# W0 product moved into the first gather's tiles, second layer's weights behind the second gather

## The reference, cut to what matters

```
n    = ln(x)                                             # (6250, 256)
agg  = segment_sum((n @ W_r[type])[src] / deg[type, dst], dst)
x1   = x + agg + n @ W0.T + W0_b                         # first graph layer
x2   = x1 + moe(ln(x1))                                  # 8 experts, top 1, capacity 977
m    = ln(x2)
h    = m @ W                                             # second graph layer
x3   = x2 + leaky_relu(segment_sum over edges and self loops of dinv[src]*dinv[dst]*h[src] + b, 0.2)
out  = x3 + lstm_block(ln(x3))                           # one LSTM along the nodes, two attention sums
```

## Time and profile before

| | us |
|---|---|
| median of three runs (4289.60 to 4295.48) | 4293.77 |
| the profiled execution | 4290.27 |
| its span in the trace | 4287.7 |
| TensorE busy in it | 3575.4 (83%) |
| GpSimd busy in it | 1636.3 (38%) |
| relations, 43 to 832 us | 789 |
| first gather, 843 to about 1927 us | 1084 |
| experts, 1927 to 2388 us | 461 |
| combine, 2394 to 2508 us | 114 |
| second gather, 2508 to 3532 us | 1024 |
| LSTM, from 3539 us | 748 |

### The profile page before, as it was taken

One profiled execution on the slowest core, in us unless ns is written; L12 is line 12 of the kernel. 1 busy time (PEld: TensorE's weight loads), 2 busy tenths in 40 slices (PEclk: granted clock), 3 DMA queues, 4 the chain that ended last, 5 costly groups with the idle time before them and its releaser, 6 DMA issues. The chain is left out here.

```text
span 4287.7 us, 61539 instructions
## 1 busy us (share of the span) xinstructions
PE 3575.4 (83%) x19781; PEld 2791.4 (65%) x19781; DVE 1847.8 (43%) x5651; ACT 900.6 (21%) x2499; POOL 1636.3 (38%) x1757
## 2 busy tenths in 40 slices
PE   6999999888887787769999655667677779999996
PEld 3555444477777677756666545555555559999996
DVE  4445400134444444542333642233445554444687
ACT  2333333200000011112222310000000003444453
POOL 1000000177777777750000357777777750000000
PEclk9999999977777887769999887887888899999998
DMA  5333343333444444432221443444455554433333
GB/s 218 135 127 135 119 171 150 134 112 113 114 116 117 118 118 121 120 94 91 82 82 51 141 154 104 121 133 137 150 159 172 171 173 147 154 109 114 108 108 108
DMA packets 213143, 546.88 MB, mean 128 GB/s; under 512 B 42849, under 2 KB 111310, under 8 KB 197975
## 3 DMA queue, kind: packets, MB, share of 16 engines
q1 hardware_dynamic: 125448, 301.92, 20.8%
q0 software_dynamic: 83344, 235.84, 18.9%
q10 hardware_dynamic: 4032, 5.24, 0.4%
HBM read 363.45 MB, written 178.97 MB: 127 GB/s over the span
## 5 line engine op out<-in xcount | busy, mean ns | idle before, releaser
L1672 POOL DMA_INDIRECT b_msg<-scratch_gtab,k_src_row x784 | 762.2, 972 | 267.9 <-issue 260.9
L932 POOL DMA_INDIRECT a_msg<-scratch_hrel,k_rel_row x784 | 751.5, 959 | 240.8 <-issue 236.5
L1721 PE MATMUL b_ps<-b_hit,b_msg 128*128 128x128 f32 x3136 | 497.4, 325 | 299.1 <-DMA b_msg<-scratch_gtab,k_src_row 290.6
L996 PE MATMUL a_ps<-a_hit,a_msg 128*128 128x128 f32 x3136 | 558.0, 351 | 195.3 <-DMA a_msg<-scratch_hrel,k_rel_row 186.9
L1721 PEld LDWEIGHTS b_ps<-b_hit,b_msg 128*128 128x128 f32 x3136 | 465.4, 235 | 362.3 <-issue 277.6
L713 PE MATMUL r_psm<-k_w,r_xnT 128*128 128x512 f32 x1568 | 693.7, 596 | 3.3 <-ACT r_hst L671 2.4
L996 PEld LDWEIGHTS a_ps<-a_hit,a_msg 128*128 128x128 f32 x3136 | 518.0, 258 | 227.6 <-DVE a_hit L1102 114.7
L2099 PE MATMUL l_psg<-k_hall,k_whhT 128*128 128x128 f32 x4672 | 566.2, 279 | 5.6 <-DVE k_hall L2216 5.4
L2099 PEld LDWEIGHTS l_psg<-k_hall,k_whhT 128*128 128x128 f32 x4672 | 543.6, 193 | 13.3 <-DVE k_hall L2216 5.9
L713 PEld LDWEIGHTS r_psm<-k_w,r_xnT 128*128 128x128 f32 x1568 | 292.0, 191 | 334.7 <-issue 331.5
L671 ACT COPY r_hst<-r_psm 128x512 f32<-128x512 f32 x392 | 229.4, 586 | 417.3 <-PE r_psm L713 417.3
(11 more groups left out here) (267 smaller groups left out, 3698.3 us busy)
## 6 DMA issues: line engine op xcount, KB each, us to landing
scratch_hrel<-r_hst SPq DMA_DIRECT2D x98, 1024.0 KB
l_xr<-scratch_xrow SPq DMA_DIRECT2D x146, 512.0 KB, 3.6
scratch_xrow<-n_xs SPq DMA_DIRECT2D x50, 512.0 KB, 3.1
a_msg<-scratch_hrel,k_rel_row POOLq DMA_INDIRECT x784, 2.8
b_msg<-scratch_gtab,k_src_row POOLq DMA_INDIRECT x784, 2.8
scratch_buf<-k_zpad POOLq DMA_DIRECT2D x8, 1056.0 KB, 7.3
scratch_ybuf<-x_ys POOLq DMA_DIRECT2D x8, 1024.0 KB
x_xr<-scratch_buf SPq DMA_DIRECT2D x7, 1056.0 KB, 5.4
```

What stands on the lines that cost most here:

```text
L932: pool.indirect_dma_start(msg[:, q, j], None, table, bass.IndirectOffsetOnAxis(ap=rows_of[:, g, j:j + 1].bitcast(U32), axis=0)).then_inc(s ...
L996: mm = pe.matmul(ps[:, u, kk, 0:WIN], msg[:, g % SL, j, kk * P:(kk + 1) * P], hit[:, u, j], start=(j == 0), stop=(j == PER - 1))
L1672: pool.indirect_dma_start(msg[:, q, j], None, k.gtab, bass.IndirectOffsetOnAxis(ap=k.src_row[:, g, j:j + 1].bitcast(U32), axis=0)).then_in ...
L1721: mm = pe.matmul(ps[:, u, kk, 0:WIN], msg[:, g % SL, j, kk * P:(kk + 1) * P], hit[:, u, j], start=(j == 0), stop=(j == PER - 1))
```

## The change

W0's product leaves the relations stage. That stage now stores each `xnT` tile to a new scratch tensor `xnt`, and GpSimd clears the whole of `accT`. The first gather loads `xnt` back (`xw`), up to four tiles ahead, and `turn_sums` adds two matmuls (`xw` against `w0`) into the same PSUM row that holds the transposed sums; the bias is added by VectorE to the loaded x. In the combine stage the W product is gone: ScalarE writes the normed row times `dinv` straight into the table (`xs`), TensorE transposes that row and ScalarE puts it into `accT` as the node's own share. In the second gather W multiplies the finished sums (`weighted` in place of `turn_sums`); the load of `gb`, its addition and the memset are gone.

```diff
 stage_edges
-                pe.wait_ge(s_w0, 32)
+                pe.wait_ge(s_w0, 16)
-                    act.dma_start(k.biasT[:], W0_b.rearrange("(a p) -> p a", p=P)).then_inc(s_w0, 16)
 stage_relations, sync: store(t, u)
+                        rest(k, sp, S["xt"], t + 2)
+                        sp.dma_start(k.xnt[bass.ds(t * P, P)], xnT[:, u].rearrange("p k t -> p (k t)")).then_inc(s_n[u], 16)
 gpsimd
+                    pool.memset(k.accT[:], 0.0).then_inc(S["z"], 1)
                     pool.wait_ge(S["xn"], 1)
 scalar: turn, tile
+                        rest(k, act, s_n[u], 16 * n + 16)
-                        for a in range(2):
-                            hold(k, act, S["b"], t + 1)
-                            ins = act.activation(k.accT[:, a, bass.ds(t * P, P)], psb[:, a * P:(a + 1) * P],
-                                                 ACT.Identity, bias=k.biasT[:, a:a + 1])
-                        ins.then_inc(S["eb"], 1)
 tensor: tile
-                        rest(k, pe, S["eb"], t + 1)
-                        for a in range(2):
-                            for kk in range(2):
-                                mm = pe.matmul(psb[:, a * P:(a + 1) * P], w0[:, kk, a * P:(a + 1) * P], xnT[:, u, kk],
-                                               start=(kk == 0), stop=(kk == 1))
-                        mm.then_inc(S["b"], 1)
 stage_first, sync: load(t)
                         sp.dma_start(xb[0:r, t % XR], x[t * P:t * P + r]).then_inc(s_x[t % XR], 16)
+                        sp.dma_start(xw[:, t % XR].rearrange("p k t -> p (k t)"), k.xnt[t * P:(t + 1) * P]).then_inc(s_x[t % XR], 16)
+                    sp.dma_start(bias[:], W0_b.partition_broadcast(P)).then_inc(S["ld"], 16)
 tensor: turn_sums(t)
+                        pe.wait_ge(s_x[t % XR], 32 * (t // XR + 1))
                         for kk in range(2):
-                            mm = pe.transpose(psa[:, kk * P:(kk + 1) * P], k.accT[:, kk, t * P:(t + 1) * P], k.ident[:])
+                            pe.matmul(psa[:, kk * P:(kk + 1) * P], k.accT[:, kk, t * P:(t + 1) * P], k.ident[:],
+                                      start=(kk == 0), stop=(kk == 1), is_transpose=True, skip_group_check=True)
+                        for kk in range(2):
+                            mm = pe.matmul(psa[:, 0:D], xw[:, t % XR, kk], k.w0[:, kk], start=False, stop=(kk == 1),
+                                           skip_group_check=True)
 vector: rows(t)
+                        v.tensor_tensor(xb[:, t % XR], xb[:, t % XR], bias[:], ALU.add).then_inc(S["xw"], 1)
+                        v.wait_ge(S["xw"], t + 1)
                         v.wait_ge(S["tp"], t + 1)
 stage_combine, scalar
-                def turn(t): ...        # xnT from pst
-                def table(t): ...       # gs = psm * dinv
+                    act.activation(xs[:, t % XR], xo[:, t % XR], ACT.Identity, bias=rstd[:, t % 2, 3:4],
+                                   scale=rstd[:, t % 2, 2:3]).then_inc(S["xn"], 1)      # norm(t), every slot
+                def own(t):
+                    act.wait_ge(S["tp"], t + 1)
+                    act.copy(tile(t), halves(pst[:, t % 2, 0:2 * P])).then_inc(S["own"], 1)
 vector: scale(t)
+                    v.tensor_tensor(rstd[:, u, 2:3], rstd[:, u, 1:2], k.dinv[:, t:t + 1], ALU.mult).then_inc(S["r"], 1)
 tensor
-                def product(t): ...     # two matmuls with w
 stage_second, sync
+                    sp.dma_start(wg[:], W.rearrange("(k p) o -> p k o", p=P)).then_inc(S["w"], 16)
-                        sp.dma_start(gb[0:r, t % XR], k.gtab[t * P:t * P + r]).then_inc(s_x[t % XR], 16)
 tensor: weighted(t) in place of turn_sums(t)
-                            mm = pe.transpose(psa[:, t % 2, kk * P:(kk + 1) * P], k.accT[:, kk, t * P:(t + 1) * P], k.ident[:])
+                            mm = pe.matmul(psa[:, t % 2, 0:D], k.accT[:, kk, t * P:(t + 1) * P], wg[:, kk],
+                                           start=(kk == 0), stop=(kk == 1))
 vector: rows(t)
-                        v.tensor_tensor(z[:, u], psa[:, u, 0:D], gb[:, t % XR], ALU.add).then_inc(S["z"], 1)
-                        link(v.scalar_tensor_tensor(out=z[:, u], in0=z[:, u], scalar=k.dinv[:, t:t + 1], in1=bs[:],
+                        v.scalar_tensor_tensor(out=z[:, u], in0=psa[:, u, 0:D], scalar=k.dinv[:, t:t + 1], in1=bs[:],
-                        v.memset(k.accT[:], 0.0).then_inc(s_z, 1)
```

More of the change, by code:

```diff
@@ L177, in _ @@
                 link(pool.memset(k.win_f[:], 0.0))
-                link(pool.memset(k.accT[:, :, k.NR * P:k.NP], 0.0))
                 cuts = [0] + [g for g in range(1, NG) if k.settled[g] != k.settled[g - 1]] + [NG]
@@ L239, in _ @@
                 act.dma_start(w0raw[:], W0_w.rearrange("(a p) i -> p a i", p=P)).then_inc(s_w0, 16)
-                with nc.allow_non_contiguous_dma("one bias of each column"):
-                    act.dma_start(k.biasT[:], W0_b.rearrange("(a p) -> p a", p=P)).then_inc(s_w0, 16)
                 for u in range(4):
@@ L745, in stage_relations, with stage_first @@
         for_windows(k, "deg", deg.window, ended, lambda: run(True))
-def stage_first(k, x, gate_w, gate_b, table, rows_of):
+def stage_first(k, x, W0_b, gate_w, gate_b, table, rows_of):
     nc, D, NG, NT, EX = k.nc, k.D, k.NG, k.NT, k.EX
@@ L1528, in _, with stage_second @@
             def _(pe):
-                def turn(t):
-                    pe.wait_ge(s_n[t % 2], t // 2 + 1)
+                for t in range(NT):
+                    pe.wait_ge(S["xn"], t + 1)
                     if t >= 2:
-                        pe.wait_ge(S["xt"], t - 1)
+                        pe.wait_ge(S["own"], t - 1)
                     for kk in range(2):
-                        mm = pe.transpose(pst[:, t % 2, kk * P:(kk + 1) * P], xn[:, t % 2, kk * P:(kk + 1) * P], k.ident[:])
+                        mm = pe.transpose(pst[:, t % 2, kk * P:(kk + 1) * P], xs[:, t % XR, kk * P:(kk + 1) * P], k.ident[:])
                     mm.then_inc(S["tp"], 1)
-                def product(t):
-                    pe.wait_ge(S["xt"], t + 1)
-                    if t >= 2:
-                        pe.wait_ge(S["ev"], t - 1)
-                    for kk in range(2):
-                        mm = pe.matmul(psm[:, t % 2, 0:D], xnT[:, t % 2, kk], w[:, kk], start=(kk == 0), stop=(kk == 1))
-                    mm.then_inc(S["mm"], 1)
-                pe.wait_ge(S["w"], 16)
-                for m in slots:
-                    if 0 <= m - 3 < NT:
-                        product(m - 3)
-                    if 0 <= m - 2 < NT:
-                        turn(m - 2)
 ORDER = (0, 2, 4, 6, 1, 3, 5, 7)
-def stage_second(k, b, W_ih, b_ih, b_hh, W_hh):
+def stage_second(k, W, b, W_ih, b_ih, b_hh, W_hh):
     nc, D, NG, NT = k.nc, k.D, k.NG, k.NT
@@ L1655, in _ @@
                             sums(i, q)
-            clear(k, [s_p, s_mm, s_add, s_z, *(s for m in s_m for s in m)])
+            clear(k, [s_p, s_mm, s_add, *(s for m in s_m for s in m)])
         def tiles(along):
@@ L1870, in _ @@
                             add(g)
-        for_windows(k, name, scan, ended=lambda: tiles(False), fixed=lambda: tiles(True), fresh=True, flag=k.late)
+        for_windows(k, name, scan, ended=lambda: tiles(False), fixed=lambda: tiles(True), flag=k.late)
 def stage_lstm(k, W_lin, b_lin, fw, bw, out):
```

136 lines of the change are left out of this document (59 added, 77 removed).

## The result

The changed kernel takes 4225.55 us, median of four runs (4219.40 to 4226.96), against 4291.69 (4289.42 to 4295.48) for the kernel before: the ratio is 0.9843, with a 95% interval of 0.9832 to 0.9855. The forecast was 4228, with 4210 to 4256 as its range.

What follows compares the result with a forecast made beforehand. TensorE was taken to bound the relations, GpSimd's indirect DMAs both gathers, a ring the combine stage. The terms -44.8 + 3 - 24.9 + 1 = -65.7 us took 4290.3 to 4224.6; with 3.5 for the median, 4228, range 4210 to 4256.

Steps and rivals of the forecast that it cites:

- The bounds by stage: Whole kernel: TensorE busy 786.4 of 789 us in relations, GpSimd's indirect DMAs pacing both gathers, a ring in the combine stage.
- 28 x 1.00 + 20 x 0.89: Relations stage: the removed product saves 1.00 us in tiles with degree counts and 0.89 without, 45.8 us.
- What is late next is VectorE in the 28 tiles: Relations, tiles with counts: VectorE needs 14.5 us against a tile of about 15.7, holding with 1 us to spare.
- the first tiles run slower: Relations stage: slower first tiles, for which 1 us is given back, making the gain 44.8 us.
- The memset of 12800 columns is done by GpSimd beside the first tile ... 0: Relations start: GpSimd has nothing else due, so clearing there costs 0; VectorE needed 10.7 us for it.
- + 3: First gather with its tail: the added work costs 3 us in the sum.
- the 2 us: First gather: 49 more VectorE additions cost GpSimd's issues 2 us; the second gather loses as many, so 0 in sum.
- -18.7 rate, -6.2 tail: Combine stage: a tile takes 1.60 us instead of 1.99, gaining 18.7 us; its end gains 6.2, together 24.9.
- +1: Second gather: W's matmuls replace two transposes per tile, hidden except in the last tiles: +1 us, bounds -2 and +4.
- full hold by VectorE's additions: First gather rival: VectorE's added work fully blocks GpSimd, 49 x 0.42 = 20 us, kernel at 4248; chance 0.07.
- half the gain: Relations and combine rival: VectorE holds counted tiles, stores or landings hold the combine at 1.8 us; 4252, chance 0.13.
- Rival 1: First gather: TensorE becomes the bound, kernel slower; about 4497 at clock 0.5, 4355 at 0.56; chance 0.03.

Runs made afterwards that it cites:

- w0_ten: The changed kernel with each of W0's matmul pairs in the first gather issued ten times instead of once: 4351.87 us, ratio 1.0148 to the kernel before.
- after: The changed kernel itself, with the whole change against the kernel before: 4225.55 us, ratio 0.9843.
- best: The changed kernel with late memset pieces, the degrees' inverse in four pieces and one small VectorE operation less per combine tile: 4202.54 us, ratio 0.9798.
- memset_edges: The changed kernel with GpSimd's memset of accT issued one stage earlier, in the edges stage: 4229.50 us, ratio 0.9861 to the kernel before.
- memset_late: The changed kernel with GpSimd's memset of accT cut into ten pieces issued late in the relations stage: 4219.26 us, ratio 0.9836.
- bias_five: The changed kernel with the bias added five times per tile instead of once, each addition waiting for the one before: 4230.03 us, ratio 0.9854.
- w0_out: The changed kernel without W0's two matmuls per tile in the first gather, the transposes kept: 4220.19 us, ratio 0.9831.

## Why the prediction was right, step by step

- **The bounds by stage** (TensorE full in the relations, GpSimd's issues in both gathers, a ring in the combine stage): right. All gains lie in the first and third, as the earlier trace rows had it.
- **Relations, "28 x 1.00 + 20 x 0.89"**: mis-sized. The spacing that went is 0.90 us in both kinds of tile; the 1.00 between starts in the earlier trace rows held 0.10 us that the first work behind the counts pays and that stayed (7.13 us for 16 pieces there, 7.03 in the second half of a tile). That is 2.8 us. The lines view has W0's records busy for 54.6 us, since each runs 0.16 us past the next one's start (1.16 for 1.00, 1.05 for 0.89). "What is late next is VectorE in the 28 tiles" was wrong as a worry (the tiles are all at 15.81), and so was "the first tiles run slower" (in before the second turn is at 52.61 us, the third at 69.32, 16.71 as later); the 1 us given back was right by luck.
- **A step that was missing**: the inverse of the degrees. It stood in the trace of before as a wait of 2.4 us of TensorE for ScalarE. What is removed inside a stretch that ends with another engine's chain is no gain; two products of 0.90 us lay in it. 45.8 - 2.8 - 1.8 = 41.2 us, and in nine of the kernels above, which have this stage unchanged but for the memset, the products take 744.8 to 746.5 us, 40.9 to 42.6 less than before. The 748.1 of the changed kernel's own trace is 1.6 to 3.3 us above them, and the clock explains 1.7 us. From 779 to 782 us its trace shows a granted 0.53, and the last two tiles' products take 15.68 us; at that place w0_ten's trace shows 1.00 and 13.98 us. Of all the traces only those of after and best have the longer one:

```profile
778.86 15.68 PE L709 MATMUL r_psm<-k_w,r_xnT 128*128 128x512 f32 x32
```

```profile
777.20 13.98 PE L709 MATMUL r_psm<-k_w,r_xnT 128*128 128x512 f32 x32
```

- **"The memset of 12800 columns is done by GpSimd beside the first tile ... 0"**: failed, 3.0 us. The cover was judged by GpSimd's queue alone ("nothing else due"); what counted was which VectorE operation it meets, a scaling that took 3.80 us in place of 0.41. A hold was weighed for the bias addition alone. Only the moves of memset_edges and memset_late show the cause: in one the hold moved with the memset, in the other it went.
- **First gather, "+ 3" in the sum**: right on the idle time that hides W0, and right in size, but no run shows this term: it was the author's estimate for W0's matmuls and VectorE's addition at the end of the stage. There the trace of before has TensorE at a granted 0.50 in nine of the twelve windows of 4 us from 1848 to 1896 us, and 1885.89 - 1880.31 = 5.58 us a group against 5.0 for four issues. With W0's matmuls left out the ratio is 0.9831 against 0.9843, with intervals that overlap, and the issues take 1045.1 us against 1043.5: W0's product costs nothing that these runs can tell from 0. The tail, where the 3 us were put, is 48.5 to 52.6 us with the change (w0_ten and bias_five left out) and 49.2 and 53.5 without. But the issues take 1043.2 us or more in every kernel with the changed stage and 1040.3 and 1040.8 in the two without it, at least 2.4 us. w0_out has them too, so they belong to what it keeps: the bias addition, priced at 2 us in the prediction and at 49 x 0.03 = 1.5 by bias_five, and the loads of `xnt`, which no run takes away alone. The prediction set the 2 us off against a gain in the second gather, for an operation that now reads PSUM. In the trace of before 114 of that stage's 784 issues begin under a VectorE operation that reads PSUM (L1809, L1816, L1843), none of which takes more than 0.96 us; 130 begin under one with both inputs in SBUF (L1799, L1818, L1820, L1824), and 59 of these take more than 1.05 us, the longest 1.47.
- **Combine, "-18.7 rate, -6.2 tail"**: right in mechanism (the ring went, VectorE is next), 1.60 a tile was 1.50. The first sum's slot in the earlier trace rows plus one operation of 0.16 gives 1.52; I had put 0.2 and a further 0.05 on it for nothing that the rows show. 48 x 0.10 = 4.8 us would be the difference, of which 3.6 came, since the mean tile is at 1.52. ScalarE's "at most 0.47 each" was wrong (its row of the table, L1463, takes 0.60 us) and without effect. The end gave 5.3 of 6.2.
- **Second gather, "+1"**: measured +0.6 in this pair. Over all traces it takes 1027.4 to 1032.9 us with the change, and 1031.0 and 1034.9 without, so that these runs can't tell +1 from a small gain. W's load, given up to 2 us, delayed nothing: TensorE's first work stands 13.7 us behind the first gather, and stood 14.9 behind it. The covered memset is shown by its return.
- **Rivals**: full hold by VectorE's additions (4248) fell with bias_five; half the gain fell with the traces (no wait for VectorE in the counted tiles, 1.52 us a tile in the combine stage); TensorE as the bound came true only at ten times W0's product. Rival 1's half clock is what the trace of before shows from 1880.31 to 1885.89 us, 0.50; eight records of L983 take 2.07 us there, and 1.15 at 1004.04 us, where it shows 1.00.

The total was right to 2.5 us because the errors cancel: 6.6 us too much in the relations and their start (by the 41.2 that the other kernels bear out and the memset's 3.0), against it 2.7 too little in the combine stage, and the rest is scatter, which in this pair of traces takes 3.2 us more from the relations and what follows them and gives 6.2 us in the two gathers, the experts and the LSTM. That it comes out so near is luck.

What stays open: in single runs the way from the last product to the first gather is 12.8 to 14.3 us, and the tail of the first gather 48.5 to 53.5 us, with nothing in the edits that goes with it. Nor does a run show why the clock fell at 779 us in two traces and not in the others.

## What to carry to other kernels

Where one engine is bound and another stage has that engine waiting for data, move work from the first to the second: here its price was near nothing until the idle time was used up (up to four times the product, not at ten times), and the low granted clock of the waiting stage is no argument against it, since in these runs it rose with the work, from 0.77 to 0.94. Before a removed piece is counted per turn, look for the turns whose length another chain sets; those gave nothing here (25.25 us against 25.22). An instruction put on an idle engine is not free by that alone: look at what runs beside it, since here a memset of GpSimd of 10.77 us held an operation of VectorE of 0.41 us on the critical path until its end.
